# Feed-forward on one Trainium2 core: four instead of three of eight inner products go through PE's output projection, four instead of five through DVE's sum

## The reference, cut to what matters

```python
def _L0_ffn_ref(x, Win, bin_, W1, b1, W2, b2, Wout, bout):
    s = jnp.einsum('btd,dm->btm', x, Win) + bin_          # m = 64
    h = jax.nn.relu(s[..., None] * W1 + b1)               # 16 inner values for each m
    g = jnp.einsum('btmh,mh->btm', h, W2) + b2
    out = jnp.einsum('btm,md->btd', g, Wout) + bout
    return out
x = x + 0.5 * _L0_ffn_ref(_layernorm(x, axis=-1), ...)    # layers 1 and 3
```

## Time and profile before

| | |
|---|---|
| median of three runs | 1338.24 us (1337.21 to 1341.51) |
| the profiled execution | 1340.82 us, its span 1339.0 us |
| PE, DVE, ACT, POOL busy | 86%, 81%, 68%, 54% of the span |
| granted TensorE clock, mean | 0.941 of full |
| layer 1's feed-forward | about 28 to 96 us of the span |
| layer 3's feed-forward | about 292 to 355 us |

### The profile page before, as it was taken

The page is one execution under the profiler, slowest core; times in us unless marked ns, Lnnn a source line. Parts: engine busy times, 40 slices in busy tenths (PEclk is TensorE's granted clock), DMA queues, the critical chain, the costliest instruction groups (busy, mean ns, idle before and its releaser), DMA issues.

```text
span 1339.0 us, 55515 instructions
## 1 busy us (share of the span) xinstructions
PE 1146.1 (86%) x22892; PEld 943.2 (70%) x22892; DVE 1087.9 (81%) x4029; ACT 910.1 (68%) x2131; POOL 722.3 (54%) x655
## 2 busy tenths in 40 slices
PE   2766888877758999999998579999668999999996
PEld 1654666656637888888888357777347889888986
DVE  4976888868788899999992578888588899899981
ACT  3854555558657887888874346666557888788882
POOL 4234545443147787878875400000149788788882
PEclk9888999989859999999999889999679999999999
DMA  6000000000002222222222000000002222222223
GB/s 165 20 1 1 2 2 2 2 1 1 1 16 51 48 48 53 57 47 47 47 51 48 1 1 1 0 0 1 1 21 62 48 48 47 49 61 48 47 63 82
DMA packets 27569, 43.41 MB, mean 32 GB/s; under 512 B 6961, under 2 KB 18481, under 8 KB 27441
## 3 DMA queue, kind: packets, MB, share of 16 engines
q1 hardware_dynamic: 27440, 41.82, 14.0%
HBM read 6.15 MB, written 2.10 MB: 6 GB/s over the span
## 4 chain that ended last, share of the span: by engine, by line
PE 51%; DVE 11%; issue 9%; ACT 3%; DMA 2%; SPq 2%; POOL 1%; POOLq 0%; DVEq 0%
PE bank L1898 22%; PE bank L1880 7%; PE bank L1909 7%; PE bank L1871 4%; DMA rowsD<-work 2%; DVE work L981 2%; PE bank L1782 2%; SPq L333 2%; PE bank L1764 2%; DVE work L1023 1%; DVE work L654 1%; PE bank L1476 1%; PE bank L1727 1%; PE bank L1743 1%; PE bank L1697 1%
## 5 line engine op out<-in xcount | busy, mean ns | idle before, releaser
L1898 PEld LDWEIGHTS bank<-rowsD,work 128*32 128x32 f32 x16384 | 360.2, 194 | 56.4 <-issue 56.0
L1898 PE MATMUL bank<-rowsD,work 128*32 128x32 f32 x16384 | 371.6, 276 | 20.9 <-issue 11.9
L446 POOL TENSOR_SCALAR work<-work 128x1024 f32<-128x1024 f32 x64 | 181.7, 2840 | 127.8 <-ACT work L1349 127.7
L434 POOL TENSOR_TENSOR work<-work 128x512 f32<-128x512 f32 x128 | 167.8, 1335 | 25.4 <-ACT work L1374 19.3
L1349 ACT ACTIVATE work<-work 128x128 f32<-128x128 f32 x512 | 162.7, 412 | 1.9 <-DVE work L1043 1.9
L1357 ACT ACTIVATE work<-work 128x128 f32<-128x128 f32 x512 | 158.3, 398 | 6.0 <-DVE work L1053 6.0
L448 POOL TENSOR_TENSOR work<-work 128x1024 f32<-128x1024 f32 x64 | 152.5, 2383 | 5.3
L1023 DVE STREAM_TRANSPOSE work<-work 128x1024 f32<-128x1024 f32 x128 | 151.3, 1221 | 1.9 <-ACT work L1357 1.9
L1374 ACT ACTIVATE work<-bank 128x512 f32<-128x512 f32 x128 | 78.0, 618 | 90.8 <-PE bank L1898 90.5
L1909 PE MATMUL bank<-kout,work 128*128 128x128 f32 x1024 | 128.1, 278 | 2.8 <-POOL work L434 2.8
L1880 PE MATMUL bank<-xT,kinT 128*128 (+1 forms) x512 | 126.7, 393 | 4.5 <-ACT work L1366 4.5
(11 more groups left out here) (199 smaller groups left out, 2315.3 us busy)
## 6 DMA issues: line engine op xcount, KB each, us to landing
rowsD<-work SPq DMA_DIRECT2D x256, 128.0 KB, 2.4
x_sb<-in_L_attn_x_dram SPq DMA_DIRECT2D x8, 256.0 KB, 4.5
out_dram<-x_sb SPq DMA_DIRECT2D x4, 512.0 KB, 5.3
headsel<-in_c_headsel_dram SPq DMA_DIRECT2D x1, 512.0 KB, 4.8
work<-in_L_ffn_key_in_dram SPq DMA_DIRECT2D x1, 512.0 KB, 8.0
kout<-in_L_ffn_key_out_dram SPq DMA_DIRECT2D x4, 128.0 KB, 4.8
work<-in_L_ffn_keys_dram SPq DMA_DIRECT2D x1, 256.0 KB, 2.9
wqkv<-in_L_attn_W_qkv_dram SPq DMA_DIRECT2D x1, 192.0 KB, 4.7
```

The source lines that it names most:

```text
L434: last = nc.gpsimd.tensor_tensor(cg[:, par, :].rearrange("p (j t) -> p j t", j=NCH)[:, :, half * 64:half * 64 + 64], csb[:, par, 512 * hal ...
L446: nc.gpsimd.tensor_scalar(wmask, both, 1.0 - 5e-7, None, ALU.is_ge).then_inc(s["wm"], 1)
L1898: last = nc.tensor.matmul(bank[2 + half][k * NK:(k + 1) * NK, :] .rearrange("p (j t c) -> p t c j", j=NCH, t=16)[:, t % 16, :, :], xrows[: ...
```

## The change

JPE becomes 4. The setup makes a fourth product w2 times Wout, and the buffer w2o has four slices of 128 in place of three; DVE's sum has four relus, one tensor_scalar and three scalar_tensor_tensor for each group; PE's output projection has five matmuls for each tile, 20 for each group, in place of four and 16. ACT writes the same eight relus, j = 4 to 7 first and 0 to 3 after them. The semaphore counts follow from the constant.

```diff
 LN_EPS = 1e-5
 STAGES = 6
-JPE = 3
+JPE = 4
 SLOTS = 64
```

## The result

The changed kernel takes 1336.11 us (median of 22 runs, 1333.9 to 1340.86) against 1338.76 (22 runs) for the kernel before: the ratio is 0.9978, 95% interval 0.9969 to 0.9987, so 2.9 us faster (1.7 to 4.2), with the most likely value inside the 0.3% that I had called no change. The forecast was 1334.0, the range 1330.5 to 1338.5. That single pair shows over twice what the runs show, and most of this study is about that gap.

What follows compares the result with a forecast made beforehand. DVE's sums were taken to pace both feed-forward stages. Gains of 3.9 us in the first and 0.3 in the second, 4.2 in all, took 1340.82 to 1336.6; 2.6 lower for the runs' median gave 1334.0, range 1330.5 to 1338.5.

Steps and rivals of the forecast that it cites:

- What bounds the kernel: Both feed-forward stages: PE's projections wait for DVE's last sum, starting 0.1 us behind it, not for ACT's relus.
- rival C: DVE's end was not the pace, or attention swallows the lead: no change, 1338 us; chance 0.13.
- FFN1, up to the seventh projection: First feed-forward: first projection at 38.0, ACT the pace from 45.8, seventh projection at 73.7 instead of 77.00, 3.3 us earlier.
- The clock: First feed-forward's end: seventh projection at full clock, 4.47 us; eighth starts at half clock, 6.4 instead of 5.3; gain 3.9.
- rival B: Fuller PE stays at full clock, the first feed-forward's eighth projection saves 1.9 us more: 1332.1; chance 0.10.
- rival A: Half clock stays in the first feed-forward's seventh or eighth projection, 1.8 to 2.2 us of gain go: 1336.1; chance 0.20.
- FFN2: Second feed-forward: a wash, PE takes back what DVE gives; DVE's last update comes 0.3 us earlier.
- the lead of 3.0 us in the middle: Second feed-forward: period 6.3 us against 7.31 over three groups that DVE paces, a lead of about 3.0 us.
- The folding: Second feed-forward's last two groups, where PE folds keys: period from 6.22 to 7.1 us, the lead falls to 1.2.
- the last projection: Second feed-forward's eighth projection: starts straight behind the seventh and is itself 0.9 us longer.
- Rival D: PE becomes the pace, added products exposed in both feed-forwards, 5.6 us: slower, 1343.8; chance 0.07.
- The sum: Whole kernel: 3.9 + 0.3 = 4.2 us gain; profiled execution 1340.82 to 1336.6, less 2.6 for the runs' median, 1334.0.

Runs made afterwards that it cites:

- dve_short: Kernel before with one sum fewer on DVE per group (one relu left out of the result), PE as before: 0.9941, 1330.05 us.
- ffn1_only: Four products on PE in the first feed-forward alone, three in the second as in the kernel before: 0.9973, 1336.07 us.
- after_again: The changed kernel as it is, run again for comparison on one chip: 0.9975 to the kernel before, 1336.62 us.
- mixed: Changed kernel, but the last three groups of the second feed-forward again with three products on PE and five sums on DVE: 0.9996, 1339.08 us.
- mixed_padded: mixed with 48 semaphore increments on PE after the second feed-forward: 0.9973 to the kernel before, 1333.76 us.
- mixed_filled: mixed with 12 identity products on PE around the first feed-forward's seventh and eighth projection, no increments: 0.9947 to the kernel before, 1332.76 us.
- after_shift48: Changed kernel with 48 semaphore increments on PE behind the second feed-forward: 0.9979 to the kernel before, 1337.31 us.
- before_again: The kernel before, unchanged, in another single profiled execution: first feed-forward 60.2 us, run 1337.15 us.
- ffn2_only: Four products on PE in the second feed-forward alone, three in the first as in the kernel before: 0.9989, 1337.97 us.
- pe_long: Kernel before with one product more per PE projection block (one added twice), DVE as before with five: 1.0049, 1345.08 us.

## Why the prediction was right, and where it was off

*What bounds the kernel.* Right, and the central point. PE's projections waited for DVE's sums, not for ACT's relus; the 0.1 us distances in the earlier trace rows told more than the releaser. dve_short shows it with 7.9 us, and ffn1_only shows the gain in the stage where the forecast had it; rival C falls.

*FFN1, up to the seventh projection.* The start at 38.0 is exact (38.04). ACT restarted at 45.10, not 45.8, since the first projection took 6.0 us, not 6.6. How long it stays cold is a draw as well: 6.0 to 7.1 us in the traces with the changed FFN1. The rest of the chain, 27.9 us from there to the seventh projection, is right to a tenth (45.10 to 73.00).

*The clock.* The step that failed. I took the cold eighth projection of the earlier trace rows as the kernel's own, and expected it cold again after the change: 6.4 against 5.3 us. In the traces of the changed kernel, after_again, ffn1_only, mixed, mixed_padded, mixed_filled and after_shift48 its first part takes 1.13 to 1.28 us, so it is at full clock (4.5 us, 82.88 to 87.42), which is rival B's event; rival A's is in none of them. before_again and ffn2_only show that the code of before has it at full clock in some executions as well. The two errors partly cancel, and that is luck: FFN1's gain is 3.1 us against the executions of before whose eighth projection is warm, 6.3 in the pair of profiles, and 3.9 in the forecast. The Trainium skill ("TensorE: Matmul & The Clock Gate", section "HAM oscillation") has it that closing waits between bursts of matmuls keeps the full rate. The traces agree in part: with the changed kernel's FFN1 the seventh and eighth are warm in all seven traces, but pe_long, with as many products and DVE's sums as before, has the eighth cold behind 1.27 us of idle PE, and ffn1_only has the transposes and the attention's projection before the eighth cold (1.12 and 1.91 us) behind 2.19. With the pauses of before they are cold in one execution and warm in the next: the seventh cold in part in both traces of the kernel before, warm in ffn2_only; the eighth cold once, warm twice. That the fuller PE is what keeps the clock is not shown.

*FFN2.* "A wash" is right: forecast 0.3 us shorter, measured 0.3 to 0.4 longer in the changed kernel and after_again (0.9 in ffn2_only, 1.2 in after_shift48, whose first projections were cold longer). The mis-sized term is the lead of 3.0 us in the middle. I took 7.31 against 6.3 for three groups and left out those that DVE did not pace. In the timeline of the kernel before, ACT's third and fourth group:

```profile
310.46 5.51 ACT L1159 ACTIVATE work<-bank,b1e,w1c 128x512 f32<-128x512 f32 x8
...
316.42 5.47 ACT L1159 ACTIVATE work<-bank,b1e,w1c 128x512 f32<-128x512 f32 x8
```

They start 5.78 us behind 304.68 and 5.96 behind each other, without idle time on ACT: ACT was the pace. With PE as the pace these became 6.81 and 6.20, a loss of 1.3 against the 0.7 by which the second group was ahead: at the fourth group the changed kernel was 0.5 behind, where the forecast had it level. The three groups that DVE paced then gave 2.4, not 3.0 (7.32, 7.31 and 6.70 became 6.24, 6.45 and 6.20). By the starts of ACT's groups the lead was at most 1.9 (before the seventh group). The folding took 0.9 of it twice, as forecast (7.11 against 6.22 at ACT's eighth group, and once more at the update of the seventh), and the last projection 0.4 where the forecast had 0.9: 0.3 behind.

*Rival D* is what pe_long makes real: the added products alone cost 0.49%. It did not come about because DVE's relief is a little larger.

*The sum.* 4.2 us forecast, 2.9 measured (1.7 to 4.2). The forecast's median, 1334.0, is 2.1 us below the 1336.11 measured: 1.6 by the gain (the medians are 2.65 apart) and 0.5 by its base, the 1338.24 of three runs where 22 give 1338.76. It stood 2.6 us below the sum for the profiled execution, and that execution's FFN1 was 3.2 us longer than that of before_again; that the one explains the other is likely, not shown.

## What to carry to other kernels

When an engine waits for two others, compare when each ended with when it started; the releaser's name is no proof. A start 0.1 us behind the end of one of them points to that one, and taking work off it, as dve_short does, shows it. Moving work from the pacing engine to the next pays the difference of two chains, so walk every group of the stage, those not paced by it too; measuring each half alone shows how close the two terms are and where a split by group pays. Before a difference of under 0.5% is explained from one pair of traces, look at a second execution of the same kernel.

## What was not expected of the hardware

One and the same program has its eighth projection at half or full clock in different executions (5.4 or 3.8 us), behind the same pauses of 2.13 and 2.19 us, and its seventh likewise (3.8 us in ffn2_only). The front of the stage varies by as much: 13.25 to 15.28 us with the code of before. Together that is 3.2 us in FFN1 between two executions of the kernel before, more than the change under study. And a stage of 365 us that an edit did not touch took 370.0 in one execution of mixed; all other traces lie between 364.3 and 366.9. mixed's runs, 0.9996 against 0.9973 and 0.9947 for the two versions with 48 more instructions on PE, say that the loss is not only that execution's; what causes it is open.
